# Self attentions of a decoder kernel: heads taken out with queries in rows, and a block of unread products

## The chip, the cores and the metric

The kernel runs on one core of one Trainium2 chip. The metric is the device time of one execution, in microseconds. The kernel before took 6091.39 us (median of three runs, 6082.24 to 6093.36). The profiled execution that the trace comes from took 6097.89 us, and its instructions span 6096.0 us of them.

## The reference

The program is a decoder of four layers over a batch of 16 sequences of 100 tokens with 128 features. Each layer is a self attention, a cross attention and a feed-forward part, each on the layernormed input and added to it. Only the four self attentions change. Each has 16 heads. Three of them (layers 0, 1, 3: `sa0`, `sa1`, `sa3`) have heads of 8 features and a causal mask; their core is the same:

```python
att = softmax(where(causal, einsum('bhqd,bhkd->bhqk', q, k) * scale, -inf))
y = einsum('bhqk,bhkd->bhqd', att, v)           # 8 features for each head
x = x + out_scale * (y.transpose().reshape(B, T, C) @ w_out + b)
```

The one of layer 2 (`sa2`) is a difference of two attentions over the same values, 16 features for each head, without a mask, and with a root mean square norm for each head:

```python
att = att1 - lam * att2
y = einsum('bhts,bhse->bhte', att, v)
y = y * rsqrt(mean(y * y, axis=-1) + 1e-5) * subln_w * (1 - LAMBDA_INIT)
x = x + y.transpose(0, 2, 1, 3).reshape(B, T, 2 * C) @ c_w.T
```

## The kernel before, in words

Activations lie with the 128 features in the partitions and tokens in the columns. A self attention goes through the 16 sequences in four groups G of four. A *unit* is one group and one softmax (`sa2` has two softmaxes, `sm` 0 and 1, so eight units; the others have four). A unit has eight *steps* t, one for each half (eight heads) of one sequence: 32 steps in `sa0`, `sa1`, `sa3`, 64 in `sa2`. The order on each engine is written out by hand, and semaphores tie the engines together.

In step t TensorE (all line numbers are those of the profile) puts the mask of step t + 3 into a score bank (`mask_scores`, L2751, causal stages alone), subtracts the row maxima of step t in banks 4 and 5 (`lower`, L2763 the transposed mask and L2764 the product with the diagonal of maxima), then does what `beside` names for this step, then the scores of step t + 3 (`score`, L2757) between those of step t with keys in rows (`scoreT`, L2770), four products that lie in different row groups and run side by side. VectorE takes the maxima of step t + 3 (L1818), GpSimd makes the diagonal of it (L951), and ScalarE takes the exponential of step t (L1260). Behind its scores TensorE does `values(t - 1)` (L2786): eight products that give, for each head, the weighted values and, by a column of ones, the sum of the weights. **The first instruction of step t + 1 waits for the exponential of step t** (`probsT_ready`): banks 4 and 5 are used again at once.

Two steps fill bank 6, one *slot* (a sequence): 16 heads in blocks of 32 partitions, 8 (or 16) rows of values and one row with the sum. ScalarE copies it to `o_sb` (`keep`, L1213). Then, in odd steps, `gathered` (L2795, four products whose stationary side is `o_sb` and whose moving side has 4 columns) turns the sums into a 100 x 16 tile in bank 7, VectorE inverts them (`inverse`, L1827), ScalarE writes each inverse 32 times (`widen`, L1227), and in even steps `spread` (L2804, four products of 128 x 100) brings the inverses back under their rows, where VectorE multiplies (`normalise`, L1837, L1839). `project` (L2820) is four products of 128 x 400 for a group, since the heads are spread over four blocks with gaps. In `sa2` the root mean square goes the same way: `squared` on ScalarE (L1218), `mean_squares` (L2795 again), `roots` (L1223), `widen_roots`, four `scale` for a group (L2804 again) and L1864 on VectorE. Value rows of the next group (L2740 the bias, L2741) are made in four steps of a unit, between `lower` and the scores. All these share bank 7, which goes back by `proj_free`.

The stage ends with a tail that has no scores of following steps: the last slots pass through `gathered`, `inverse`, `widen`, `spread` and `normalise` one after another, then the last `project` and `update` (L1874, L1876, L1878), which the next layernorm waits for. `sa1` also rounds its weights on VectorE before it starts (`quantise`, L1653), its output weight of 512 columns among them.

## Time and profile before

| | |
|---|---|
| median of three runs | 6091.39 us |
| profiled execution / its span | 6097.89 / 6096.0 us |
| TensorE busy | 4686.6 us (77%) |
| VectorE, ScalarE, GpSimd busy | 3317.4, 2411.6, 2210.9 us |
| `sa0`, GpSimd's diagonal of step 3 to that of step 31 | 81.02 to 232.93 us |
| `sa1`, the same | 1997.39 to 2110.84 us |
| `sa2`, step 3 to step 63 | 2655.21 to 2975.25 us |
| `sa3`, step 3 to step 31 | 4443.66 to 4573.51 us |

A busy TensorE is one that has a product under way; how fast the product goes depends on the clock that it is granted, which the profile gives as a share of full speed for each stretch (1.00 is 2.4 GHz, 0.50 is 1.2 GHz; it has no other level, so 0.72 is a mix in time). The chain of waits on the page has nothing on these stages; they are read from windows and from the timeline.

### The profile page before, as it was taken

To read this page: it belongs to the slowest core of one execution; us is meant where nothing else is said; L and a number is where in the kernel's file an instruction comes from. 1 tells how busy PE (TensorE), PEld (TensorE's weight loads), DVE (VectorE), ACT (ScalarE), POOL (GpSimd) and SP (SyncE) were. 2 spreads that over 40 slices of the span, in tenths; PEclk is the share of its full clock that TensorE was granted. 3 is DMA by queue.
4 is the path that set the end of the run, shared out by engine and by line. 5 is a ranking of instruction groups with operands and counts; after the bars stand their busy time and mean duration, and the time that the engine had idled before them with its cause. 6 is when DMAs were issued, how large, how long until landed. Compare 5 with 4: busy or idle time off the path is not lost. (4 is left out here: it accounts for less than half of the span.)

```text
span 6096.0 us, 84213 instructions
## 1 busy us (share of the span) xinstructions
PE 4686.6 (77%) x22350; PEld 3081.4 (51%) x22350; DVE 3317.4 (54%) x4953; ACT 2411.6 (40%) x3566; POOL 2210.9 (36%) x1247
## 2 busy tenths in 40 slices
PE   8899999999798966689878888888495444431698
PEld 4578888888544545346545555555252222220344
DVE  3344444444345322443266665664636999987344
ACT  2255555555222311233235555554133555540122
POOL 1256666555100300022146666664032555540000
PEclk6799999999799967775578998998686666655699
DMA  2000000000011022200021211110000000000011
GB/s 76 1 8 16 16 16 16 16 16 8 16 43 43 1 51 51 61 8 1 1 54 41 46 40 42 40 40 19 0 1 21 21 22 22 22 16 0 11 43 37
DMA packets 125094, 153.15 MB, mean 25 GB/s; under 512 B 87424, under 2 KB 110736, under 8 KB 124592
## 3 DMA queue, kind: packets, MB, share of 16 engines
q1 hardware_dynamic: 124720, 148.82, 10.0%
q8 instruction: 154, 2.52, 0.2%
q14 instruction: 220, 1.80, 0.1%
HBM read 110.42 MB, written 2.66 MB: 19 GB/s over the span
## 5 line engine op out<-in xcount | busy, mean ns | idle before, releaser
L1050 POOL TENSOR_TENSOR pexp_lo<-arena,pexp_hi 128x800 fp32r<-128x800 f32 x384 | 727.6, 1895 | 433.4 <-POOLq L1049 432.4
L1005 POOL TENSOR_TENSOR pexp_lo<-arena,pexp_hi 128x800 fp32r<-128x800 f32 x384 | 637.3, 1660 | 466.9 <-POOLq L1004 466.9
L2205 DVE TENSOR_REDUCE arena<-ps 100x1 f32<-100x482 f32 (+1 forms) x768 | 477.5, 656 | 235.7 <-DVEq L2174 223.3
L2060 DVE TENSOR_REDUCE arena<-ps 128x1 f32<-128x482 f32 (+3 forms) x624 | 392.8, 656 | 381.6 <-DVEq L2038 370.2
L1348 ACT ACTIVATE arena<-ps 128x800 f32<-128x800 f32 x384 | 322.3, 839 | 511.7 <-ACTq L1346 509.7
L1414 ACT ACTIVATE arena<-ps 128x800 f32<-128x800 f32 x384 | 321.8, 838 | 415.4 <-ACTq L1408 408.0
L951 POOL TENSOR_TENSOR max_diag<-w_const,arena 100x800 fp32r<-100x800 f32 x160 | 245.3, 1533 | 614.1 <-POOLq L949 614.1
L3202 PE MATMUL ps<-kst,qs 96*100 96x482 f32 (+1 forms) x768 | 338.3, 442 | 109.9 <-PEq L3162 105.7
L2512 DVE MATCH_REPLACE8 arena<-arena 100x1444 f32<-100x1444 f32 x256 | 420.3, 1652 | 0.0
L3440 PE MATMUL ps<-arena,chunk 128*128 128x400 f32 x648 | 285.2, 522 | 71.8 <-PEq L3439 71.1
L3344 PE MATMUL ps<-w_const,w_cross 100*128 100x100 f32 x192 | 43.2, 380 | 374.5 <-PEq L3341 374.5
L1818 DVE TENSOR_REDUCE arena<-ps 100x8 f32<-100x800 f32 x160 | 158.6, 992 | 307.0 <-DVEq L1815 306.8
L1349 ACT ACTIVATE pexp_hi<-ps 128x800 fp32r<-128x800 f32 x384 | 319.5, 832 | 0.0
L1415 ACT ACTIVATE pexp_hi<-ps 128x800 fp32r<-128x800 f32 x384 | 319.3, 832 | 0.0
L1089 POOL TENSOR_TENSOR arena<-arena 100x1444 f32<-100x1444 f32 x64 | 207.8, 3247 | 285.1 <-POOLq L1088 285.1
L2502 DVE MAX8 arena<-arena 100x8 f32<-100x1444 f32 x192 | 309.5, 1656 | 0.0
L2602 DVE TENSOR_TENSOR arena<-ps,arena 128x400 f32<-128x400 f32 x256 | 146.9, 574 | 293.5 <-DVEq L2593 184.4
L946 POOL MEMSET minus_ones<- 100x100 f32 x4 | 0.7, 182 | 833.7 <-POOLq L945 833.7
L1590 ACT ACTIVATE arena<-ps 128x400 f32<-128x400 f32 x256 | 129.0, 504 | 424.0 <-ACTq L1587 423.7
L3094 PE MATMUL ps<-pexp_hi,ctxk_hi 128*97 128x400 f32 (+1 forms) x768 | 281.2, 366 | 15.8 <-PEq L3089 15.6
L3432 PE MATMUL ps<-xn,chunk 128*128 128x400 f32 x648 | 278.6, 513 | 0.0
L3075 PE MATMUL ps<-qa_hi,ctxT_hi 113*128 113x400 f32 (+1 forms) x768 | 276.4, 360 | 1.4 <-PEq L3069 1.4
(365 smaller groups left out, 10880.3 us busy)
## 6 DMA issues: line engine op xcount, KB each, us to landing
ctxT<-in_ctxT SPq DMA_DIRECT2D x64, 541.5 KB
ctxk<-in_ctx SPq DMA_DIRECT2D x48, 528.0 KB
kst<-mid SPq DMA_DIRECT2D x128, 180.5 KB, 3.1
chunk<-in_ff_chunks SPq DMA_DIRECT2D x77, 193.0 KB, 2.4
arena<-gate_dram SPq DMA_DIRECT2D x64, 200.0 KB, 3.1
kst<-xn SPq DMA_DIRECT2D x64, 180.5 KB, 2.9
arena<-gate_dram SPq DMA_DIRECT2D x64, 100.0 KB, 2.6
w_cross<-in_ca SPq DMA_DIRECT2D x1, 3728.5 KB, 12.5
```

The source lines that it names most:

```text
L1005: own(nc.gpsimd.tensor_tensor(pexp_lo[p % 3][:, :, :], pexp[p % 3], pexp_hi[p % 3][:, :, :], ALU.subtract))
L1050: own(nc.gpsimd.tensor_tensor(pexp2_lo[p % 3][:, :, :], pexp2[p % 3], pexp2_hi[p % 3][:, :, :], ALU.subtract))
L1348: nc.scalar.activation(pexp[p % 3], of, ACT.Exp, scale=scale).then_inc(s.pexp_ready, 1)
L1349: own(nc.scalar.activation(pexp_hi[p % 3][:, :, :], of, ACT.Exp, scale=scale))
L1414: nc.scalar.activation(pexp2[p % 3], of, ACT.Exp, scale=scale).then_inc(s.pexp_ready, 1)
L1415: own(nc.scalar.activation(pexp2_hi[p % 3][:, :, :], of, ACT.Exp, scale=scale))
L2060: peak = nc.vector.tensor_reduce(mparts[0:at.stop - at.start, m, c:c + 1], bank(k, z - a, at.stop - at.start), AX.X, ALU.max)
L2205: peak = nc.vector.tensor_reduce(mparts2[:, h, c:c + 1], bank(k, z - a, S), AX.X, ALU.max)
L2502: nc.vector.max(tops[:, k, at], left[k]).then_inc(done[i], 1)
L2512: nc.vector.match_replace(left[k], tops[:, k, at], scores_sb[i] if r == 0 else left[k], TAKEN).then_inc(done[i], 1)
L3202: ins = mm(bank(k, z - a, S), qs[par][0:C, g, S * (h % 4):S * (h % 4) + S], kst[0:C, g, a:z], start=True, stop=True)
L3440: ins = mm(bank(4 + g), chunk[c][:, 256:384], h_all[k], start=False, stop=last)
```

## The change

The heads leave `o_sb` another way. `gathered` now has a moving side that picks all the rows, values and sum, of the four heads of a block: 36 columns for heads of 8 and 68 for heads of 16, so one set of four products gives a tile with the 100 queries in rows and, for each head, its features and its sum beside each other. VectorE inverts the sums and multiplies there. `inverse`, `widen` and `spread` are gone, and of `sa2` also `squared`, `mean_squares`, `widen_roots` and `scale`: squares, their sums, the product with the inverse roots and that with the weights are VectorE's, with queries in rows (`by_roots`, `by_weights`). For a group the result is turned back once (`features`, one set of four products for 128 features, so two in `sa2`), copied by ScalarE, and projected with one product (`sa2`: two). The output weight is 128 (256) columns wide, not 512. Value rows move behind `values` of even steps. In `sa2` these are steps 0, 2, 4, 6 of the units with `sm` 0. Ahead of step 0 of each stage TensorE does 14 products of 100 x 400 in bf16 (`unread`), which write banks 4 and 5 and are read by nobody.

```diff
-    own_block = i[:, None] // 32 == np.arange(4)[None, :]
+
+    def head_rows_of(n):
+
+        at = np.arange(4 * n)
+        return (i[:, None] == (at // n * 32 + at % n)[None, :]).astype(np.float32)
+
...
-                sum8=(own_block & (i[:, None] % 32 == 8)).astype(np.float32),
-                sum16=(own_block & (i[:, None] % 32 == 16)).astype(np.float32),
-                squares16=(own_block & (i[:, None] % 32 < 16)).astype(np.float32),
+                rows8=head_rows_of(9), rows16=head_rows_of(17),
...
@@ -628,38 +621,18 @@
     def beside(nsm, t):
 
         u, k = divmod(t, 8)
...
+        G, sm = u // nsm, u % nsm
+        if k % 2 == 0 and sm == 0 and G < NG - 1:
+            return "values", G + 1, k // 2
+        after = {(1, 0, 3): ("features", 0), (1, 0, 5): ("project", 0), (2, 0, 7): ("features", 0), (2, 1, 1): ("features", 1),
+                 (2, 1, 3): ("project", 0)}.get((nsm, sm, k))
+        return (after[0], G - 1, after[1]) if after and G > 0 else (None, 0, 0)
+
+    def step_behind(nsm, t):
+
+        return t % 16 if nsm == 2 and t >= 16 else -1
+
+    UNREAD_FIRST, UNREAD = 14, 0
...
+            def features(c):
+                act.wait_ge(s.proj_full, 1)
+                act.sem_inc(s.proj_full, -1)
+                nc.scalar.activation(y_feat[:, GT * c:GT * c + GT], bank(7), ACT.Copy).then_inc(s.act_done, 1)
+                act.wait_ge(s.act_done, 1)
+                act.sem_inc(s.act_done, -1)
+                act.sem_inc(s.proj_free, 1)
+                act.sem_inc(s.y_feat_ready, 1)
...
@@ -1817,54 +1766,39 @@
                 mx = smax[:, t % 3, :].rearrange("p (c h) -> p c h", c=2)
                 nc.vector.tensor_reduce(mx, sc, AX.X, ALU.max).then_inc(s.maxima_there, 1)
 
-            def norm_there():
+            def normalise(slot):
+
+                u, i = divmod(slot, 4)
+                G, sm, w = u // nsm, u % nsm, 16 * vw
+                y = y_tok[:, G % 2, w * i:w * i + w]
                 dve.wait_ge(s.norm_full, 1)
                 dve.sem_inc(s.norm_full, -1)
-
-            def inverse():
-
-                norm_there()
-                done(nc.vector.reciprocal(rden[:, :], bank(7, 16, S)))
-                dve.sem_inc(s.proj_free, 1)
-                dve.sem_inc(s.inverse_there, 1)
-
-            def normalise(slot):
-                u, i = divmod(slot, 4)
-                G, sm = u // nsm, u % nsm
-                y = y_rows[G % 2][:, :, i, :]
-                norm_there()
-                if sm == 0:
-                    done(nc.vector.tensor_tensor(y, o_sb[slot % 2], bs(bank(7)), ALU.mult))
-                else:
-                    done(nc.vector.tensor_tensor(second, o_sb[slot % 2], bs(bank(7)), ALU.mult))
-                dve.sem_inc(s.o_sb_free, 1)
+                o = bank(7, 16 * (vw + 1), S).rearrange("p (h w) -> p h w", w=vw + 1)
...
+                done(nc.vector.reciprocal(rden[:, :].unsqueeze(2), o[:, :, vw:vw + 1]))
+                r = rden[:, :].unsqueeze(2).to_broadcast([S, 16, vw])
+                to = y if sm == 0 else second
+                done(nc.vector.tensor_tensor(to.rearrange("p (h w) -> p h w", w=vw), o[:, :, 0:vw], r, ALU.mult))
                 dve.sem_inc(s.proj_free, 1)
                 if sm == 1:
-                    done(nc.vector.scalar_tensor_tensor(y, second, col[:, 6:7], y, ALU.mult, ALU.add))
-                    dve.sem_inc(s.rms_sum, 1)
+                    done(nc.vector.scalar_tensor_tensor(y, second, col[0:S, 6:7], y, ALU.mult, ALU.add))
+                    done(nc.vector.tensor_tensor(y_sq, y, y, ALU.mult))
+                    done(nc.vector.tensor_reduce(rms[:, 16 * i:16 * i + 16], y_sq.rearrange("p (h w) -> p h w", w=16), AX.X, ALU.add))
+                    if i == 3:
+                        dve.sem_inc(s.rms_sum, 1)
                 elif nsm == 1 and i == 3:
                     dve.sem_inc(s.y_ready, 1)
 
-            def mean_squares(i):
-                norm_there()
-                done(nc.vector.tensor_copy(rms[:, 16 * i:16 * i + 16], bank(7, 16, S)))
-                dve.sem_inc(s.proj_free, 1)
-                if i == 3:
-                    dve.sem_inc(s.rms_sum, 1)
-
-            def rms_inverse():
+            def by_roots(G):
+                y = y_tok[:, G % 2, :].rearrange("p (h w) -> p h w", w=16)
                 dve.wait_ge(s.rms_root, 1)
                 dve.sem_inc(s.rms_root, -1)
                 done(nc.vector.reciprocal(rms[:, :], rms[:, :]))
-                dve.sem_inc(s.inverse_there, 1)
-
-            def scale(G, i):
-                y = y_rows[G % 2][:, :, i, :]
-                norm_there()
-                done(nc.vector.scalar_tensor_tensor(y, y, subln[:, 0:1], bs(bank(7)), ALU.mult, ALU.mult))
-                dve.sem_inc(s.proj_free, 1)
-                if i == 3:
-                    dve.sem_inc(s.y_ready, 1)
+                done(nc.vector.tensor_tensor(y, y, rms[:, :].unsqueeze(2).to_broadcast([S, 64, 16]), ALU.mult))
+
+            def by_weights(G):
+                y = y_tok[:, G % 2, :].rearrange("p (h w) -> p h w", w=16)
+                done(nc.vector.tensor_tensor(y, y, subln[:, :].unsqueeze(1).to_broadcast([S, 64, 16]), ALU.mult))
+                dve.sem_inc(s.y_ready, 1)
 
...
@@ -2788,37 +2710,36 @@
                 if half == 1:
                     ins.then_inc(s.o_full, 1)
 
-            def gathered(of, which):
+            def gathered(slot):
 
                 side_bank()
+                n = 4 * (vw + 1)
                 for g in range(4):
-                    ins = mm(bank(7, 4, S, 4 * g), of[:, g, :], W("const", which), start=True, stop=True)
+                    ins = mm(bank(7, n, S, n * g), o_sb[slot % 2][:, g, :], W("const", "rows%d" % vw), start=True, stop=True)
                 ins.then_inc(s.norm_full, 1)
 
-            def spread(of):
-
+            def features(G, c):
                 side_bank()
-                pe.wait_ge(s.inverse_wide, 1)
-                pe.sem_inc(s.inverse_wide, -1)
-                for g in range(4):
-                    ins = mm(bank(7, S, 128, S * g), of[:, 128 * g:128 * g + 128], ident[0:S, 0:S], start=True, stop=True)
-                ins.then_inc(s.norm_full, 1)
-
-            def mean_squares():
-                pe.wait_ge(s.head_sq, 1)
-                pe.sem_inc(s.head_sq, -1)
-                gathered(y_sq, "squares16")
-
-            def scale(i):
-                spread(rms_wide[:, 512 * i:512 * i + 512])
-
-            def project(G):
+                if c == 0:
+                    pe.wait_ge(s.y_ready, 1)
+                    pe.sem_inc(s.y_ready, -1)
+                for i in range(4):
+                    at = 16 * vw * i + 128 * c
+                    ins = mm(bank(7, S, 128, S * i), y_tok[:, G % 2, at:at + 128], ident[0:S, 0:S], start=True, stop=True)
+                ins.then_inc(s.proj_full, 1)
+
+            def project():
                 side_bank()
-                pe.wait_ge(s.y_ready, 1)
-                pe.sem_inc(s.y_ready, -1)
-                for g in range(4):
-                    ins = mm(bank(7), wo[:, 128 * g:128 * g + 128], y_rows[G % 2][:, g, :, :], start=g == 0, stop=g == 3)
+                pe.wait_ge(s.y_feat_ready, nsm)
+                pe.sem_inc(s.y_feat_ready, -nsm)
+                for c in range(nsm):
+                    ins = mm(bank(7), wo[:, 128 * c:128 * c + 128], y_feat[:, GT * c:GT * c + GT], start=c == 0, stop=c == nsm - 1)
                 ins.then_inc(s.out_full, 1)
+
+            def unread(n):
+
+                for i in range(n):
+                    mm(bank(4 + i % 2, GT, S), id_bf, causal_bf[:, :], start=True, stop=True)
 
...
@@ -2848,6 +2769,8 @@
                 if t % 8 == 0:
                     pe.wait_ge(s.q_diag_ready, 1)
                     pe.sem_inc(s.q_diag_ready, -1)
+                if t % 8 == 0:
+                    unread(UNREAD if t > 0 else UNREAD_FIRST)
                 if more:
                     pe.wait_ge(s.scores_read, 1)
```

How the rows of TensorE stand in step 4 of `sa1` (an even step), before; the line numbers are those of each kernel's own text:

```order
L2764 MATMUL ps<-max_diag_49,minus_ones 100x400
L2741 MATMUL ps<-w_sa,xn 100x128
L2757 MATMUL ps<-arena 100x400
L2770 MATMUL ps<-arena 100x400
L2757 MATMUL ps<-arena 100x400
L2770 MATMUL ps<-arena 100x400
L2804 MATMUL ps<-w_const,arena 128x100 x4
L2786 MATMUL ps<-arena 32x100 x8
```

and now:

```order
L2686 MATMUL ps<-max_diag_50,minus_ones 100x400
L2679 MATMUL ps<-arena 100x400
L2692 MATMUL ps<-arena 100x400
L2679 MATMUL ps<-arena 100x400
L2692 MATMUL ps<-arena 100x400
L2708 MATMUL ps<-arena 32x100 x8
L2663 MATMUL ps<-w_sa,xn 100x128
```

L2757 is L2679 now (scores), L2770 is L2692 (scores with keys in rows), L2786 is L2708 (values), L2741 is L2663 (value rows), L2804 is `spread`. The value rows went from ahead of the scores to behind `values`, and `spread` is gone.

TensorE in step 13 of `sa1` (the odd step that projects group 0), before:

```order
L2764 MATMUL ps<-max_diag_50,minus_ones 100x400
L2763 MATMUL ps<-causalT_bf,ident_bf 100x400
L2764 MATMUL ps<-max_diag_50,minus_ones 100x400
L2820 MATMUL ps<-deviation,w_sa 128x400 x4
L2757 MATMUL ps<-arena 100x400
L2770 MATMUL ps<-arena 100x400
L2757 MATMUL ps<-arena 100x400
L2770 MATMUL ps<-arena 100x400
L2786 MATMUL ps<-arena 32x100 x8
L2795 MATMUL ps<-w_const,squares 100x4 x4
```

and now:

```order
L2686 MATMUL ps<-max_diag_50,minus_ones 100x400
L2685 MATMUL ps<-causalT_bf,ident_bf 100x400
L2686 MATMUL ps<-max_diag_50,minus_ones 100x400
L2736 MATMUL ps<-mid,w_sa 128x400
L2679 MATMUL ps<-arena 100x400
L2692 MATMUL ps<-arena 100x400
L2679 MATMUL ps<-arena 100x400
L2692 MATMUL ps<-arena 100x400
L2708 MATMUL ps<-arena 32x100 x8
L2718 MATMUL ps<-w_const,squares 100x36 x4
```

L2820 was four projection products and L2736 is one; L2795 was `gathered` with 4 moving columns and L2718 is the same with 36. The turn back (L2728, four products of 128 x 100) stands in step 11, at the place that the projection has here.

VectorE in `sa2`, two steps of a unit with `sm` 1, before (L1818 maxima, L1827 inverse, L1839 and L1843 the second softmax, L1850 the mean squares):

```order
L1839 TENSOR_TENSOR squares<-squares,ps 128x400
L1843 SCALAR_TENSOR_TENSOR deviation<-squares,col,deviation 128x4x100
L1818 TENSOR_REDUCE arena<-ps 100x8
L1827 RECIPROCAL arena<-ps 100x16
L1850 COPY arena<-ps 100x16
L1818 TENSOR_REDUCE arena<-ps 100x8
L1839 TENSOR_TENSOR squares<-squares,ps 128x400
L1843 SCALAR_TENSOR_TENSOR deviation<-squares,col,deviation 128x4x100
```

and now (L1767 maxima, L1777 inverse, L1780 and L1783 the second softmax, L1784 squares, L1785 their sums for each head):

```order
L1784 TENSOR_TENSOR deviation<-arena 100x256
L1785 TENSOR_REDUCE arena<-deviation 100x16
L1767 TENSOR_REDUCE arena<-ps 100x8 x2
L1777 RECIPROCAL arena<-ps 100x16
L1780 TENSOR_TENSOR squares<-ps,arena 100x256
L1783 SCALAR_TENSOR_TENSOR arena<-squares,col,arena 100x256
L1784 TENSOR_TENSOR deviation<-arena 100x256
L1785 TENSOR_REDUCE arena<-deviation 100x16
```

Where two steps had an inverse, two operations of 128 x 400 and a copy, they have an inverse and four operations on tiles of 100 x 256, one behind another.

## Rows read from the trace of the kernel before

**Rows 1.** The head of the page.
```profile
span 6096.0 us, 84213 instructions
```

**Rows 2.** Windows, diagonal 3 to last: stretch, us, PE, PEld, DVE, ACT, POOL, PEclk.
```profile
81.02:232.93 151.91, 147.99 (x1112) 89.69 (x1112) 46.78 (x69) 48.43 (x78) 42.69 (x29) 0.72 0.00 1
1997.39:2110.84 113.45, 106.36 (x1088) 68.51 (x1088) 48.61 (x67) 47.91 (x80) 42.70 (x29) 0.97 0.01 2
2655.21:2975.25 320.04, 307.32 (x2227) 195.14 (x2228) 118.33 (x183) 123.01 (x191) 91.47 (x60) 0.60 0.01 1
4443.66:4573.51 129.85, 123.16 (x1112) 75.73 (x1112) 49.24 (x69) 48.02 (x80) 42.70 (x29) 0.88 0.01 2
```

**Rows 3.** Windows: inside `sa0`, inside `sa1`, and twice inside `sa2`.
```profile
95.00:165.00 70.00, 69.94 (x404) 42.19 (x404) 15.78 (x24) 19.35 (x32) 15.25 (x10) 0.50 0.00 1
2010.00:2110.00 100.00, 95.07 (x996) 62.38 (x992) 45.08 (x61) 42.85 (x71) 38.12 (x25) 1.00 0.01 2
2666.00:2700.00 34.00, 31.00 (x369) 18.72 (x358) 20.56 (x27) 19.18 (x31) 15.74 (x11) 1.00 0.01 1
2705.00:2800.00 95.00, 91.75 (x635) 59.01 (x635) 33.35 (x54) 35.16 (x55) 25.76 (x17) 0.55 0.00 1
```

**Rows 4.** TensorE in `sa1` at 2.4 GHz: start, us, operation, tiles, count, [idle].
```profile
2060.34 0.51 PE L2751 MATMUL ps<-causal_bf,ident_bf 100*100 100x400 bf16 x2 [0.19 <-PEq L2853]
...
2062.35 1.14 PE L2804 MATMUL ps<-w_const,arena 100*128 100x100 f32 x8
...
2063.42 0.55 PE L2786 MATMUL ps<-arena 100*32 100x100 f32 x16
...
2066.64 0.87 PE L2795 MATMUL ps<-w_const,squares 128*100 128x4 f32 x8
...
2067.54 0.51 PE L2751 MATMUL ps<-causal_bf,ident_bf 100*100 100x400 bf16 x2
```

**Rows 5.** TensorE in `sa0` at 1.2 GHz, the timeline.
```profile
126.24 1.50 PE L2795 MATMUL ps<-w_const,squares 128*100 128x4 f32 x8
...
127.60 0.89 PE L2751 MATMUL ps<-causal_bf,ident_bf 100*100 100x400 bf16 x2
...
131.35 2.03 PE L2804 MATMUL ps<-w_const,arena 100*128 100x100 f32 x8
```

**Rows 6.** TensorE in `sa2` at 1.2 GHz, the timeline.
```profile
2854.07 0.97 PE L2764 MATMUL ps<-max_diag,minus_ones 100*100 100x400 f32 x2
...
2856.57 2.03 PE L2804 MATMUL ps<-w_const,arena 100*128 100x100 f32 x8
...
2859.35 0.99 PE L2764 MATMUL ps<-max_diag,minus_ones 100*100 100x400 f32 x2
```

**Rows 7.** ScalarE in `sa1`: the first exponential's table, and a later exponential.
```profile
1996.15 1.28 ACT L1260 ACT_TABLE_LOAD   x1 [3.46 <-ACTq L1259]
...
2062.61 0.84 ACT L1260 ACTIVATE arena<-ps 100x800 f32<-100x800 f32 x1 [1.05 <-ACTq L1259]
```

**Rows 8.** TensorE in `sa1`: step 1, and the last projection inside the steps.
```profile
1998.58 0.51 PE L2751 MATMUL ps<-causal_bf,ident_bf 100*100 100x400 bf16 x2 [2.60 <-PEq L2853]
...
2111.75 2.92 PE L2820 MATMUL ps<-deviation,w_sa 128*128 128x400 f32 x8
```

**Rows 9.** VectorE in `sa2`: an update beside GpSimd's work, maxima, an update alone.
```profile
2696.66 1.25 DVE L1843 SCALAR_TENSOR_TENSOR deviation<-squares,col,deviation 128x400 f32<-128x400 f32 x1 [0.33 <-DVEq L1763]
...
2708.93 0.99 DVE L1818 TENSOR_REDUCE arena<-ps 100x8 f32<-100x800 f32 x1 [1.82 <-DVEq L1815]
...
2976.85 0.63 DVE L1843 SCALAR_TENSOR_TENSOR mid<-squares,col,mid 128x400 f32<-128x400 f32 x1 [0.33 <-DVEq L1763]
```

**Rows 10.** VectorE: the last update of `sa1`, and that of `sa2`.
```profile
2138.24 0.57 DVE L1878 TENSOR_TENSOR x<-ps,x 128x400 f32<-128x400 f32 x1 [5.29 <-DVEq L1871]
...
3037.83 0.57 DVE L1878 TENSOR_TENSOR x<-ps,x 128x400 f32<-128x400 f32 x1 [6.27 <-DVEq L1871]
```

**Rows 11.** VectorE, rounding the output weight of `sa1`.
```profile
1976.71 0.69 DVE L1675 TENSOR_TENSOR w_sa<-squares,w_sa 128x512 f32<-128x512 f32 x1
```

168 lines of the change are left out of this document (41 added, 127 removed).

## The prediction

> **What bounds the kernel now.** The head of the page comes first: the span is 6096.0 us [rows 1] of the 6097.9 that the profiled execution took, and the median of the runs is 6.5 us below that. The chain of waits has nothing on the self attentions, so I cut each of them out by windows, from GpSimd's diagonal of step 3 to its last one: 28 steps in `sa0`, `sa1`, `sa3`, 60 in `sa2`. They take 151.9, 113.5, 129.9 and 320.0 us [rows 2]. Three stages with the same instructions differ by a third, and the column beside them tells why: the granted clock is 0.72, 0.97 and 0.88, and 0.60 in `sa2`. TensorE is busy for 94 to 97% in all four, while VectorE, ScalarE and GpSimd are busy for less than half. So TensorE sets the pace, and what it costs depends first on its clock.
>
> Smaller windows show the two levels apart [rows 3]. `sa0` from 95 to 165 is at 1.2 GHz (0.50) with TensorE busy for 69.94 of 70 us. `sa1` from 2010 to 2110 is at 2.4 GHz (1.00) with 95.07 of 100. `sa2` is at 2.4 GHz from 2666 to 2700, then at 0.55 for the next 95 us. A full engine is thus no guard of the clock.
>
> Now one step. At 2.4 GHz two steps of `sa1` go from mask to mask in 2067.54 - 2060.34 = 7.20 us, of which `spread` is 1.14, `values` 0.55 and `gathered` 0.87 [rows 4]. At 1.2 GHz mask to `spread` is 131.35 - 127.60 = 3.75 us instead of 2.01, `spread` 2.03, `gathered` 1.50 [rows 5]. In `sa2` at 1.2 GHz a step with `spread` is 2859.35 - 2854.07 = 5.28, and 2.50 of it lie ahead of `spread` [rows 6].
>
> There is a second limit just below TensorE's work, a ring: step t + 1 may not begin before the exponential of step t ends. The exponential starts 2062.61 - 2060.34 = 2.27 us behind the mask and takes 0.84; from an exponential's end to the next mask is 1998.58 - (1996.15 + 1.28 + 0.84) = 0.31 us [rows 7, 8]. The ring is 3.42 us, whatever TensorE has left to do.
>
> **The change part by part.** I work out each stage at either clock, then choose the clock.
>
> Even causal steps lose `spread` and get value rows behind `values`. Mask to the end of the scores is 2.01 and `values` 0.55: 2.56 us, so 0.86 us are free ahead of the ring's 3.42, and value rows (a product of 100 x 128, with the bias two) lie inside them. Odd steps keep 2.01 + 0.55 and `gathered`, now of 36 columns. It has no row; between 0.87 (4 columns) and 1.14 (100 columns, `spread`) it is 0.96 by proportion, together 3.5. A pair of steps is 6.9 us. 14 pairs are 97. For each of three groups one turn back (as `spread`, 1.14) and one projection product (a quarter of 2.92 [rows 8], 0.73) add 5.6. With 1.3 for the first exponential's table, which lies in the window, a causal stage at 2.4 GHz is 104 us. At 1.2 GHz the ring is 3.75 + 0.26 + 0.84 + 0.31 = 5.16, an odd step 3.75 + 0.83 (between 0.55 and its double) + 1.68 = 6.26; 14 pairs are 160, with 3 x 3.5 and the table 172 us.
>
> The clock. `sa1` is at 2.4 GHz already, and its steps stay as dense: -9.5. In `sa0` the clock rises only past 165, behind the first projection of four wide products, which the change takes away; in its place 14 wide products without a wait between them stand ahead of the steps. I take it that they raise the clock at the start, as the projection did, and that steps with 0.86 us idle in 6.9 hold it, as `sa1` held it with 5 us idle in 100 [rows 3]: `sa0` 104 (-48), `sa3` 108 with a piece at 1.2 (-22). This is the choice that weighs most, and the bounds are 104 and 172 for each stage.
>
> The Trainium skill ("TensorE: Matmul & The Clock Gate", "What's actually happening") says that the throttled clock is the default and that activity releases it. [...]
>
> The block itself: two masks are 0.51 us at 2.4 [rows 4] and 0.89 at 1.2 [rows 5], so 14 products are 3.6 or 6.2 us. TensorE may be waiting there anyway for the first diagonal; each stage pays 0 to 6.2. I take 3.7 and 15 for four.
>
> `sa2` at 1.2 GHz: the ring is 2.50 + 0.26 + 0.84 + 0.31 = 3.91, an odd step with `gathered` of 68 columns (1.50 to 2.03, 1.85) is 2.50 + 0.83 + 1.85 = 5.18. 60 steps at 4.55 are 273; six turns back (12.2) and three double projections (each half of four products at half the clock, 2.92, 8.8), 294; with 9 for three changes of ScalarE's tables for the root (1.28 a load [rows 7], two loads each and what waits for them), 303. At 2.4 GHz the ring without masks is 3.42 - 0.51 = 2.91 and units with `sm` 0 run at 3.0. In those with `sm` 1 VectorE may be the bound: two maxima (0.99 each), an inverse, and four operations on 256 columns. One of 400 takes 1.25 us beside GpSimd's work and 0.63 alone [rows 9], so one of 256 is 0.4 to 0.8; with 0.33 of wait ahead of each of five, two steps are 5.5 to 7.1, and I take 3.6 for one. On average 3.3: 198, with turns, projections and tables 219. Its clock falls now at 2700 while it is well filled, and the change makes its steps no denser, nor has it a block later than the first. I take one part in five at 2.4 GHz, as 0.60 says now: 0.8 x 303 + 0.2 x 219 = 286, that is -34, between 0 (all at 1.2 with VectorE late in its `sm` 1 units) and -101.
>
> "SBUF — State Buffer", "Who interferes with whom", of the Trainium skill says that VectorE's operations with two inputs in SBUF and GpSimd's lock each other out. The trace agrees, 1.25 against 0.63 us; it bears on three of the new operations in two steps of `sm` 1.
>
> The tails. `sa1` goes from 2110.84 to the last update, 2138.81 [rows 10], 28.0 us. Twice an inverse, a widening, `spread` (1.14) and their hand-overs stand in it, and a projection of 2.92. A `spread` with a ScalarE operation and two hand-overs of 0.3 is about 2.3; both go, the projection loses 2.2, and a turn back with its copy costs 2.1: -4.7; at the clocks of the other stages up to -9. I take -6.5, -7.5, -7.5, in all -22 (bounds -12 and -28). `sa2` takes 3038.40 - 2975.25 = 63.1. Four rounds of `scale` (2.03 + 0.63 + 0.6 = 3.3) and of squares with their gathering (1.50 + 0.84 + 0.6 = 2.9) go, 25 us, and operations on VectorE of 0.4 to 1.6 come, seven of them, while a chain of widening goes: -25 with bounds -15 and -35.
>
> The output weight is rounded in 128 columns instead of 512: one such operation takes 0.69 [rows 11]; of five, three quarters go, -2 (0 if the stage's start waits for something else).
>
> Sum: -48 - 9.5 - 22 - 34 - 22 - 25 - 2 + 15 = -147.5. 6097.9 - 147.5 is 5950.4, and with the 6.5 us that the median lies below the profiled execution, 5944. What is late next is the exponential in even causal steps, TensorE in odd ones and in `sa2`.
>
> **The rivals.**
>
> A, the forecast: 5944.
>
> B, `sa2` also holds 2.4 GHz. For it: its steps lose the long thin products, as `spread`, and it held the level for 34 us with the table and VectorE's work as they are. Against: it lost it behind a filled stretch, and gets no block there. It gives 219 instead of 286: 5877.
>
> C, one causal stage does not rise or falls back. For it: `sa0` stands at 0.50 for 70 us with a full engine, and its projection, behind which the clock rose, is gone; the first exponential's table leaves TensorE 2.60 us idle [rows 8] right behind the block in `sa1` and `sa3`. Against: `sa1` rose by itself at 2007, `sa3` at 4475 without any projection. 172 instead of 104: 6012; for two of them 6080.
>
> D, slower: none of the four holds the clock, since the ring now leaves 0.86 us idle in each even step and 2.60 behind the block. It decides at the granted clock of steps 1 to 8: at 0.50 there, nothing later lifts it. 3 x 68 - 4 for `sa3`, 17 in `sa2`, and 2.5 more for each block: 5944 + 227 = 6171, 80 over the median of before. `sa1`, at 1.00 with the same ring, speaks against it.
>
> E, the change does not do what it says for the clock: block and denser work leave it as it is in each stage. At the mix of 0.72 (44 parts in 100 at 2.4 GHz) `sa0` is 1 / (0.44/104 + 0.56/172) = 133, `sa3` at 0.88 in the same way 115: 36 more than A, 5980. If also VectorE takes all of `sa2`'s gain (34) and the tails stay at their low bounds (20), 6034. For it: `sa1` and `sa3` rose with what they have, so the block may only come early. Against: nothing that I can read.
>
> **How the numbers follow.** A 0.48, own range 5910 to 5980; B 0.20; C 0.17; E 0.10; D 0.05. The range leaves out D, two stages of C and what lies under B: 5865 to 6030. 0.2% is 12 us, about what a measurement of this kernel can tell from no change. Faster is A, B, C and most of E: 0.92; within 0.2% 0.03 (two stages of C with a tail at its bound); slower 0.05, D.
>
> **What the profile after would show.** Windows as in rows 2: 104, 104, 286 and 108 us at 1.00, 1.00, 0.60 and 0.95. Mask to mask over two causal steps 6.9 us, even steps with 0.9 us idle ahead of the mask and an exponential as its releaser, `gathered` 0.96 at 2.4 GHz. The block 3.6 us long and behind it 2.60 idle in `sa1`. In `sa2` `gathered` 1.05 or 1.85, VectorE's share above the 37% of now (118.33 of 320.04), most in `sm` 1. Tails 21.5 and 38 us. I am wrong if a causal stage stands at 0.50 past its step 8 (C, D), if `sa2` is above 0.8 (B), or if VectorE is what ends TensorE's waits in `sa2`.

## The result, and the profile after

The changed kernel takes 5865.53 us (median of four runs, 5842.36 to 5872.14) against 6092.38 for the one before: the ratio is 0.9617, with a 95% interval of 0.9581 to 0.9653. That is faster by some 227 us where 147 were forecast. The direction, the causal stages and the tails came out as worked out or somewhat better; one term, the clock of `sa2`, was mis-sized by most of the difference. It is close to rival B (5877). The median lies at the very edge of the range (5865), and 0.9617 of the 6091.39 that the forecast started from is 5858, just below it.

The profiled execution took 5872.14 us. The head of its page:

```profile
span 5870.4 us, 81917 instructions
```

Windows of the kernel after, from the diagonal of step 3 to the last, `sa0`, `sa1`, `sa2`, `sa3`. The columns are the stretch, its us, the busy time of TensorE, its weight loads, VectorE, ScalarE and GpSimd, then the granted clock. They answer to [rows 2].

```profile
83.77:183.59 99.82, 94.76 (x1018) 57.11 (x1017) 42.10 (x69) 41.12 (x68) 42.69 (x29) 1.00 0.01 2
1928.97:2033.60 104.63, 94.86 (x996) 56.43 (x996) 41.01 (x67) 40.43 (x71) 42.69 (x29) 0.95 0.01 2
2593.56:2822.00 228.44, 193.16 (x1895) 103.48 (x1896) 126.64 (x196) 93.25 (x145) 93.70 (x61) 0.81 0.01 1
4255.73:4356.94 101.21, 94.88 (x1018) 57.27 (x1018) 42.09 (x69) 41.16 (x71) 42.69 (x28) 1.00 0.01 2
```

The stages are shorter by 52.1, 8.8, 91.6 and 28.6 us, 181.1 together. In `sa2` read the busy time and the clock together. TensorE was idle for 12.7 of 320.0 us before (320.04 - 307.32) and is for 35.3 of 228.4 now, and yet its clock went from 0.60 to 0.81. An engine with nearly three times the idle time got the higher clock.

The last updates on VectorE, `sa1` and `sa2`, answer to [rows 10]:

```profile
2051.53 0.57 DVE L1812 TENSOR_TENSOR x<-ps,x 128x400 f32<-128x400 f32 x1 [5.20 <-DVEq L1805]
...
2849.79 0.57 DVE L1812 TENSOR_TENSOR x<-ps,x 128x400 f32<-128x400 f32 x1 [9.39 <-DVEq L1805]
```

From the last diagonal these tails are 17.9 us (27.4 to the same point before) and 27.8 (62.6), so 9.5 and 34.8 us less. The tails of `sa0` and `sa3` are 18.8 us (30.6 before) and 19.6 (29.6), so 11.8 and 10.0 less. Stages and the tails of `sa1` and `sa2` make 225 us, as much as the spans differ; the blocks at the starts, the other two tails and what differs between the stages about cancel. Among these is a thing that the change does not touch: the cross attention and the feed-forward part between `sa1` and `sa2` took 509.8 us before and 534.7 now.

```profile
2138.24:2648.03 509.79, 329.65 (x1403) 224.70 (x1403) 173.59 (x321) 80.67 (x168) 26.83 (x34) 0.72 0.21 51
```

is the window of the kernel before, and of the one after:

```profile
2051.53:2586.24 534.71, 355.82 (x1403) 244.29 (x1403) 173.52 (x321) 80.62 (x168) 26.81 (x33) 0.66 0.19 48
```

The same 1403 products at 0.66 instead of 0.72 took 25 us more. In the run e1 below, with the same code there, the stretch took 509.5 us. Over all the profiles of this document it falls into two groups: 508 to 510 us at 0.72 (the kernel before, e1, e2, e6, e9) and 531 to 536 us at 0.66 or 0.67 (all others). All three profiles with the steps of before are in the first group, and only two of the eleven with the new steps; whether that is chance or comes from what stands ahead of the stretch, no run here tells. One profile of a kernel is therefore read stage by stage, and a stage's time has some chance in it.

TensorE of the kernel after in `sa1` at 2.4 GHz, an even and an odd step: start, us, line, tiles, and the idle time before it in brackets. They answer to [rows 4].

```profile
1986.70 0.51 PE L2673 MATMUL ps<-causal_bf,ident_bf 100*100 100x400 bf16 x2 [0.22 <-PEq L2776]
...
1989.18 0.46 PE L2663 MATMUL ps<-w_sa,xn 128*100 128x128 f32 x2
1990.09 0.51 PE L2673 MATMUL ps<-causal_bf,ident_bf 100*100 100x400 bf16 x2 [0.44 <-POOLq L923]
...
1992.57 0.90 PE L2718 MATMUL ps<-w_const,squares 128*100 128x36 f32 x8
1993.51 0.51 PE L2673 MATMUL ps<-causal_bf,ident_bf 100*100 100x400 bf16 x2
```

The last diagonal on GpSimd and the exponential on ScalarE that stand ahead of the second mask, and a mask behind an even step that makes no value rows:

```profile
1986.59 1.52 POOL L924 TENSOR_TENSOR max_diag<-w_const,arena 100x800 fp32r<-100x800 f32 x1 [1.86 <-POOLq L922]
1988.96 0.84 ACT L1211 ACTIVATE arena<-ps 100x800 f32<-100x800 f32 x1 [2.76 <-ACTq L1210]
...
2019.08 0.51 PE L2673 MATMUL ps<-causal_bf,ident_bf 100*100 100x400 bf16 x2 [0.84 <-POOLq L923]
```

Mask to mask is 3.39 us for the even step and 3.42 for the odd one: 6.81 for both, where 7.20 stood and 6.9 was forecast. `gathered` with 36 columns takes 0.90 us; with 4 it took 0.87. Nine times the columns go through for 0.03 us more. Keep this pair in mind for e9 below.

The block, once in `sa0`, where it starts at the lower clock, and once in `sa1`:

```profile
75.06 4.91 PE L2742 MATMUL ps<-causal_bf,ident_bf 100*100 100x400 bf16 x14
...
1923.12 2.54 PE L2742 MATMUL ps<-causal_bf,ident_bf 100*100 100x400 bf16 x14 [0.21 <-PEq L2771]
```

And in `sa2` the first place behind its start where its clock falls, ScalarE's table loads around the root first:

```profile
2650.97 1.28 ACT L1197 ACT_TABLE_LOAD   x1 [0.46 <-ACTq L1196]
...
2652.63 1.28 ACT L1211 ACT_TABLE_LOAD   x1
```

and TensorE's rows there, `gathered` of step 3 of group 1 and `lower` of step 4:

```profile
2651.24 0.92 PE L2718 MATMUL ps<-w_const,squares 128*100 128x68 f32 x8
2655.21 0.96 PE L2686 MATMUL ps<-max_diag,minus_ones 100*100 100x400 f32 x2 [3.04 <-PEq L2783]
```

Behind an idle time of 3.04 us the same `lower` takes 0.96 us instead of 0.58: the engine is at 1.2 GHz. The falls of units 4 and 6 stand at 3.41 and 3.38 us of the same kind. The fall behind the first root lasts 7 us, those behind the second and the third 37 us each: windows of unit 4 and unit 5, around the second.

```profile
2690.72:2718.32 27.60, 22.02 (x242) 11.20 (x241) 21.68 (x31) 14.50 (x22) 12.97 (x9) 0.89 0.01 2
2718.32:2757.68 39.36, 36.42 (x270) 20.54 (x269) 14.43 (x25) 11.95 (x19) 12.19 (x8) 0.60 0.00 1
```

### The profile page after: what moved, and what is told of

Same layout as the page of the kernel before. It is cut to its first block and busy times, and to the rows that moved or that the text cites. A ratio compares the mean times of both kernels' runs of the same rounds, so it can differ in the third digit from the quotient of the medians.

```text
span 5870.4 us, 81917 instructions
## 1 busy us (share of the span) xinstructions
PE 4451.6 (76%) x21582; PEld 2913.4 (50%) x21582; DVE 3299.6 (56%) x4961; ACT 2348.7 (40%) x3474; POOL 2212.0 (38%) x1247
## 5 line engine op out<-in xcount | busy, mean ns | idle before, releaser
L1767 DVE TENSOR_REDUCE arena<-ps 100x8 f32<-100x800 f32 x160 | 158.3, 991 | 248.2 <-DVEq L1764 248.1
```

## The experiments

My theory before the first of them: the block brings the clock up at each start, the denser steps hold it, and in `sa2` the absence of `spread` and its like (thin products: 100 columns and fewer for each stationary side) keeps it up. The rivals: the steps need no block; the clock of `sa2` hangs on the root's tables; the place of the value rows. Stage times below are the same windows as above, from one profile of each kernel; medians and ratios are from the timed runs.

**e1, without the block.**

```diff
-    UNREAD_FIRST, UNREAD = 14, 0
+    UNREAD_FIRST, UNREAD = 0, 0
```

> The changed kernel without the 14 unread products. Theory 1 (the block brings the clock up at each stage's start, the denser steps hold it): sa0 has nothing that lifts it and stays at 1.2 GHz for most of its 28 steps, about 170 us instead of 99.8; sa3 comes late as before, 20 us more; sa1 and sa2 alike within 10; in all +80 to +110 us over 5865, less 11 for four blocks. Theory 2 (the denser steps lift the clock by themselves): sa0 within 115 us, the whole within 20 us of the changed kernel, or faster by the 11 us that the blocks take.

5841.06 us, ratio 0.9578 (0.9527 to 0.9628). Windows of `sa0` and `sa2`:

```profile
80.93:186.75 105.82, 101.15 (x1018) 59.97 (x1018) 42.09 (x69) 41.38 (x69) 42.68 (x29) 0.93 0.01 2
...
2574.84:2785.27 210.43, 172.86 (x1874) 92.26 (x1870) 126.63 (x195) 92.50 (x145) 95.56 (x60) 0.89 0.01 2
```

Theory 1 falls: `sa0` rises without the block, at 96 us by the profile's record of the granted clock, and loses 6 us, not 70. `sa3` takes 102.9.

**e2, the kernel before with the block alone.**

```diff
                 if t % 8 == 0:
                     pe.wait_ge(s.q_diag_ready, 1)
                     pe.sem_inc(s.q_diag_ready, -1)
+                if t == 0:
+                    for n in range(14):
+                        mm(bank(4 + n % 2, GT, S), id_bf, causal_bf[:, :], start=True, stop=True)
```

> The kernel before with the block of 14 alone ahead of each stage. Theory 1 (block lifts, what streams through the array holds): sa0 is lifted at its start and, since it held 2.4 GHz for units 2 and 3 with the same steps, keeps it: about 115 to 120 us instead of 151.9; sa3 about 117 instead of 129.9; sa2 falls at its first roots as now, 320 give or take 15: 6045 to 6055. Theory 2 (the block is worth nothing without the denser steps): within 10 us of 6091.

6061.2 us, ratio 0.9933 (0.9899 to 0.9967). `sa0`, `sa2` and `sa3`:

```profile
83.88:201.29 117.41, 110.22 (x1112) 69.24 (x1112) 49.34 (x69) 48.03 (x78) 42.67 (x29) 1.00 0.01 2
...
2633.77:2947.16 313.39, 299.83 (x2231) 191.71 (x2232) 119.68 (x184) 122.81 (x191) 91.42 (x60) 0.63 0.01 1
4416.20:4547.35 131.15, 123.66 (x1112) 76.10 (x1112) 49.32 (x69) 47.83 (x80) 42.67 (x28) 0.88 0.01 1
```

With the steps of before the block does work in `sa0` (117.4 instead of 151.9), as theory 1 has it. `sa2` gains little, 313.4 for 320.0. In `sa3` (131.2 for 129.9) the sum hides two things, the first and the last unit:

```profile
4400.32:4440.16 39.84, 35.17 (x240) 19.36 (x236) 10.11 (x14) 11.74 (x21) 12.19 (x9) 0.76 0.01 1
...
4511.55:4547.35 35.80, 34.82 (x266) 21.12 (x264) 9.62 (x14) 10.06 (x15) 10.66 (x7) 0.67 0.01 1
```

Before they took 46.24 us at 0.52 and 25.41 at 1.00. So the block lifted `sa3` early too, and then its clock fell for 24 us in the last unit, where TensorE has no idle time of even 1 us. So block and new steps each come with a mended `sa0`; their gains don't add.

**e3, no table change in `sa2`.** A copy stands in place of the square root of the mean squares.

```diff
-                nc.scalar.activation(rms[:, :], rms[:, :], ACT.Sqrt, bias=eps_col(0)[0:S], scale=1 / 16)
+                nc.scalar.activation(rms[:, :], rms[:, :], ACT.Copy, scale=1 / 16)
```

> The changed kernel whose square root of the mean squares in sa2 is left out (a copy stands in its place, so ScalarE loads no other table inside the steps). Theory 1 (the clock of sa2 falls because TensorE stands idle for 3.04 us behind the two table loads of 1.28 us each, as at 2652): sa2 is at 1.00 from its second unit on, about 200 us instead of 228, the tail shorter by 3 to 5, in all -30 to -35. Theory 2 (the clock falls by VectorE's load in units with sm 1 or by itself): the loads' own time goes, 3 x 3 us and 3 in the tail, -10 to -13, and the clock stays near 0.81.

5856.75 us, ratio 0.9588 (0.9542 to 0.9634). `sa2`:

```profile
2603.47:2815.53 212.06, 180.46 (x1896) 97.39 (x1896) 123.35 (x196) 84.33 (x139) 93.60 (x60) 0.87 0.01 2
```

Neither theory's number. The idle times of over 3 us are gone and the falls behind them too, but the clock then falls elsewhere, twice in unit 3 and once each in units 5, 6 and 7; the longest idle times there are 1.0 to 1.2 us, and one of 1.14 us in unit 1 brought none. So the long idle times are not the only end of the high clock. What they cost in all this run can't tell: r1 below has the tables and takes 207.6 us.

**e4, thin products in even steps** of all stages, where `spread` was.

```diff
+                if t % 2 == 0 and t >= 4:
+                    side_bank()
+                    for g in range(4):
+                        ins = mm(bank(7, S, 128, S * g), ident[0:S, :], ident[0:S, 0:S], start=True, stop=True)
+                    ins.then_inc(s.proj_free, 1)
                 if t > 0:
                     values(t - 1)
```

> The changed kernel with four unread products of 128 x 100 in each even step from step 4 on, where spread stood, in bank 7. Theory 1 (removing spread is what gives sa2 its clock, since little streams through the array in it): sa2 is back at 0.60 to 0.65 and takes 280 us or more instead of 228; causal stages keep 1.00 and gain at most the 0.3 us by which an even step then passes the ring, 4 to 5 us each. Theory 2 (sa2's clock comes from the shorter stage or the missing scale and squares): sa2 stays at 0.8 and takes 228 + 29 x 0.3 = 237; the whole 20 us more.

5897.15 us, ratio 0.9651 (0.9604 to 0.9699). `sa2`:

```profile
2612.94:2853.01 240.07, 224.43 (x2116) 136.96 (x2120) 126.69 (x196) 96.37 (x144) 93.58 (x60) 0.82 0.01 2
```

Against the first profile of the changed kernel theory 2 holds: 240.1 for 228.4 us with the clock where it was. `spread` cost its own time, 9.1 us in `sa0` (108.9), 8.6 in `sa3`, 12 in `sa2`, more than I gave it, since a step that holds it is longer than the ring. But against the second profile, r1 below (207.6 at 0.93), `sa2` is 32.5 us longer and its clock lower, and e7 below says the same beside e1. So whether thin products in every second step lower the clock of `sa2` is open; by these later profiles they do.

**e5 and e6, thin or wide in every step of `sa2`.** The pair differs in what the engine does for the same time.

```diff
+                if nsm == 2 and (t >= 16 or t >= 4 and t % 2 == 0):
+                    side_bank()
+                    for g in range(4):          # e5
+                        ins = mm(bank(7, S, 128, S * g), ident[0:S, :], ident[0:S, 0:S], start=True, stop=True)
+                    for g in range(6):          # e6 instead
+                        ins = mm(bank(7, GT, S), id_bf, causal_bf[:, :], start=True, stop=True)
+                    ins.then_inc(s.proj_free, 1)
```

> The changed kernel with four unread products of 128 x 100 (thin, as spread, scale and the gathering of squares were) in sa2 alone: in each even step of its first two units and in every step from 16 on, in bank 7. Theory 1 (few columns through the array for the time that they hold it: that is what kept sa2 of before at 1.2 GHz): sa2 at 0.65 or less and 290 us or more instead of 228. Theory 2 (they only cost their own time, 1.0 to 1.2 us, less what was idle): sa2 stays at about 0.8; 62 sets cost at most 70 us at that mix, of which 0.9 for each even step is free: 255 to 265.

> The same, with six unread products of 100 x 400 bf16 (1.09 us at 2.4 GHz by the block's 2.54 for 14) where e5 has four thin ones: the same engine time, but 2400 columns in place of 400. Theory 1 (what streams decides): sa2 stands at 0.95 or more and never falls for long; about 24.5 us for units 0 and 1, 31 for the others: 230 to 240 in spite of 62 blocks more. Theory 2 (busy time decides, not what the engine is busy with): the same clock and time as e5 within 10 us.

e5: 5904.46 us, ratio 0.9697 (0.9653 to 0.9742), `sa2`:

```profile
2605.71:2886.38 280.67, 270.52 (x2289) 174.43 (x2290) 117.87 (x196) 96.37 (x144) 93.54 (x61) 0.74 0.01 1
```

e6: 5853.16 us, ratio 0.9608 (0.9569 to 0.9648), `sa2`:

```profile
2574.65:2805.60 230.95, 220.18 (x2187) 122.06 (x2188) 117.36 (x196) 96.38 (x144) 93.54 (x61) 0.96 0.01 2
```

And unit 3 of each, e5 first:

```profile
2680.30:2730.55 50.25, 49.70 (x349) 33.03 (x348) 14.10 (x24) 12.16 (x19) 12.18 (x9) 0.59 0.00 1
...
2645.99:2678.53 32.54, 31.59 (x326) 18.36 (x314) 13.92 (x24) 12.16 (x19) 12.18 (x8) 1.00 0.00 1
```

This is the cleanest of the results. TensorE is busy for 96% in e5 and 95% in e6, the sets stand at the same places, and the stage with thin ones is 50 us longer; the medians of the whole differ by 51, and no run of e6 is as long as the shortest of e5 (5864.72 and 5888.33). Units 3, 5 and 7, which have them in each step and the heavier VectorE, take 50.3, 50.1 and 43.6 us with thin ones (clock 0.59 to 0.63) and 32.5, 32.9 and 30.1 with wide ones (1.00). The falls begin at the same places, the roots of units 2, 4 and 6; what differs is how long they last: 51, 48 and 38 us in e5, none, 7 and 7 in e6 (each also has one of 7 at the stage's start). Of e5's theories the second's price was too low and the first's too high: 281, between 265 and 290, at a clock of 0.74 between 0.65 and 0.8. In e6 theory 1 holds to the number, and 54 sets of work that nobody reads (the expectation of e5 has 62, which is a miscount) cost 2.5 us against the changed kernel's 228.4, and 23.4 against the 207.6 of r1. The pair doesn't say which property of the thin ones matters: they have fewer columns, but also another number type (fp32 for bf16) and more weight loads (174 us busy for 122). The columns alone are changed in e9.

**e7, thin products in even steps and no block,** the edits of e1 and e4 together.

> The changed kernel without the block, and with four unread thin products in even steps of all stages, where spread stood: the run without the block rose in sa0 at 96 us, the run with block and thin products held what it had. Theory 1 (spread's absence lets sa0 rise by itself): sa0 now stays at 1.2 GHz until group 1 or later, 140 us or more instead of 105.8, sa3 120 or more. Theory 2 (value rows, projection or the gathering let it rise): sa0 rises near 96 us again, at most 118 us.

5895.62 us, ratio 0.9676 (0.9634 to 0.9718). `sa0`:

```profile
80.77:195.36 114.59, 113.53 (x1120) 72.21 (x1120) 42.11 (x69) 42.56 (x68) 42.68 (x29) 0.93 0.01 2
```

It rises at 95.7 us again, so `spread` did not hold `sa0` down. Theory 2. In `sa2` the thin products take 27.3 us over e1's 210.4, at 0.81 for 0.89:

```profile
2614.08:2851.82 237.74, 222.45 (x2098) 136.10 (x2098) 126.24 (x195) 96.22 (x144) 94.63 (x61) 0.81 0.01 2
```

**e8, the block behind the root's tables,** and at a start in `sa0` alone.

```diff
-                if t % 8 == 0:
-                    unread(UNREAD if t > 0 else UNREAD_FIRST)
+                if t == 0 and cfg.get("gate") or step_behind(nsm, t) == 4:
+                    unread(14)
```

> The changed kernel with the block in sa0 alone of the four starts, and three more blocks of 14 in sa2 right behind the 3.04 to 3.41 us for which TensorE stands idle for the root's tables. Theory 1 (that idle is what drops the clock and a block brings it back at once): sa2's pieces at 1.2 GHz are 7 us each, the stage is 200 + 3 x 3.5 = 205 to 215 us instead of 228; three blocks at the starts saved, 8 to 10: 5830 to 5845. Theory 2 (the clock falls again by the steps themselves in units with sm 1): sa2 225 or more.

5856.14 us, ratio 0.962 (0.9578 to 0.9661). `sa2`:

```profile
2591.74:2806.26 214.52, 177.18 (x1916) 96.43 (x1912) 124.63 (x195) 92.07 (x145) 95.51 (x60) 0.92 0.01 2
```

214.5 is theory 1's number, and the falls behind the three roots lasted 3.4, 3.4 and 6.8 us; but one of 20.5 us began at 2625, ahead of the first root, and the whole is no better than the changed kernel. What it shows is less than it seems, as the repetition below tells.

**e9, the kernel before with a wider `gathered`:** 36 (68) columns stream where 4 did, and the 32 (64) more are read by nobody; each product overwrites them, so that the sums stand where they stood.

```diff
+                at, w = where["const"][which][1], {"sum8": 36, "sum16": 68}.get(which, 4)
                 for g in range(4):
-                    ins = mm(bank(7, 4, S, 4 * g), of[:, g, :], W("const", which), start=True, stop=True)
+                    ins = mm(bank(7, w, S, 4 * g), of[:, g, :], packed["const"][:, at:at + w], start=True, stop=True)
```

> The kernel before, whose gathering of sums streams 36 (68) columns instead of 4 in each of its four products; only the first 4 are read. Theory 1 (the wide gathering is what lets sa0 of the changed kernel rise by itself at 96): sa0 rises near 96 instead of 167, its window is 120 us or less instead of 151.9, sa3 gains as much as sa0 or less. Theory 2 (it is the place of the value rows or the missing waits of the chain of inverses): sa0 stays at 0.5 to about 165 and takes 2 to 4 us more.

6038.45 us, ratio 0.993 (0.9894 to 0.9965). `sa0`, `sa2`, `sa3`:

```profile
80.68:201.77 121.09, 115.15 (x1112) 71.28 (x1112) 49.24 (x69) 48.10 (x78) 42.69 (x29) 0.96 0.01 2
...
2627.17:2896.74 269.57, 248.92 (x2227) 156.43 (x2228) 128.32 (x183) 122.13 (x191) 91.49 (x61) 0.78 0.01 2
4352.97:4505.62 152.65, 147.74 (x1112) 89.50 (x1112) 47.00 (x69) 48.23 (x80) 42.68 (x28) 0.72 0.01 1
```

With an edit that only adds work, 0.03 us for a set, `sa0` is 30.8 us shorter and `sa2` 50.5, and the clock of `sa2` goes from 0.60 to 0.78 with not one instruction fewer. The whole is 0.7% faster, and its interval leaves out 1. `sa0` rises at 91.5 us. `sa3` speaks against it: it rose 100 us behind its first diagonal instead of 45, at the end of its second unit, and lost 22.8. Theory 1 for `sa0`, and not for `sa3`. These are single profiles of programs whose times spread widely (6055 to 6129 us in 13 runs of the kernel before, 6012 to 6098 in ten of e9). For `sa2` there is a second profile with the narrow set, e2's, and it agrees with the first (313.4 us at 0.63). For `sa0` without a block there is none, so its part may be chance.

**e10, without the block, value rows of group 0 back ahead of the scores** in causal stages.

```diff
+        if nsm == 1 and G == 0:
+            at = {1: 0, 3: 1, 4: 2, 6: 3}
+            return ("values", 1, at[k]) if k in at else (None, 0, 0)
         if k % 2 == 0 and sm == 0 and G < NG - 1:
             return "values", G + 1, k // 2
...
+                elif kind == "values" and nsm == 1 and t < 8:
+                    side_bank()
+                    value_rows(G, i, 7)
                 if more:
                     score(t + 3, 0)
```

> The changed kernel without the block, whose value rows of group 0 in the causal stages stand where they stood before, in steps 1, 3, 4 and 6 ahead of the scores. Theory 1 (the wide gathering lifts): sa0 rises near 96 us as without this edit, 105 to 110 us. Theory 2 (the place of the value rows lets it rise): sa0 is at 1.2 GHz up to its second group, 125 us or more.

5884.88 us, ratio 0.9673 (0.9627 to 0.9718). `sa0` and `sa3`:

```profile
79.90:186.96 107.06, 100.23 (x1022) 59.61 (x1022) 42.12 (x69) 41.35 (x69) 42.69 (x29) 0.95 0.01 2
...
4245.88:4366.13 120.25, 113.20 (x1022) 66.05 (x1022) 42.01 (x69) 41.34 (x71) 42.69 (x28) 0.82 0.01 1
```

`sa0` rises at 90.6: the place of the value rows is not what lets it. `sa3`, with nothing but the place of four pairs of products changed, rose 56 us behind its first diagonal instead of e1's 19 and took 17.4 us more than e1's 102.9. With e9 that makes two cases in which `sa3` came up late, both with the wide `gathered`; what decides when it rises is not shown.

**r1 and r2, the changed kernel and e1's kernel once more,** on one chip, in five rounds.

> The changed kernel once more, on one chip with the next run, for what its block is worth in all: 6 us gained in sa0, 3 to 4 paid in each of sa1, sa2, sa3. Theory 1 (the block is worth nothing in all): the two medians differ by less than 12 us. Theory 2 (it costs more than it brings, since where it falls sets the clock later): this one is 20 us or more above the next.

> The changed kernel without the block once more, beside the run before. Theory 1: within 12 us of it. Theory 2: 20 us or more below it, sa2 at 0.85 or more again.

5856.83 us (0.9625, 0.9588 to 0.9662) with the block and 5853.23 (0.9622, 0.9585 to 0.9659) without. Theory 1: the block is worth nothing in the whole. The 24 us by which e1 seemed better than the changed kernel are not there when both run on one chip. And `sa2` of r1, the same program as the changed kernel:

```profile
2605.54:2813.09 207.55, 169.36 (x1896) 89.96 (x1896) 127.29 (x196) 92.75 (x145) 93.70 (x60) 0.93 0.01 2
```

207.6 us and 0.93, where the first profile had 228.4 and 0.81: the 20.9 us between them are the size of chance in one `sa2`. In `sa0` of the kernel without block it was 105.8 and then 99.8, no longer than with it:

```profile
80.98:180.74 99.76, 94.76 (x1018) 57.09 (x1017) 42.12 (x69) 41.12 (x68) 42.69 (x28) 1.00 0.01 2
```

## Why the prediction came out as it did

*The bound, and the causal stages: right.* 99.8, 104.6 and 101.2 us stand where 104, 104 and 108 were forecast; the pair of steps is 6.81 for 6.9 and `gathered` 0.90 for 0.96. The ring is as I had it, 3.39 us for 3.42. An even step without value rows leaves 0.84 us idle, for 0.86; one with them leaves 0.44, since they take 0.46 of it, and the forecast of 0.9 idle ahead of the mask in every even step forgot that it had put them there. What ends that time is the exponential, as forecast. It ends at 1988.96 + 0.84 = 1989.80, and the mask starts 0.29 us later, for 0.31. The profile names GpSimd there (L923, which gives a score bank back), but by the order of the program the bank that this mask needs was given back ahead of the diagonal at 1986.59, 3.5 us earlier.

*What lifts `sa0`: right in the time, wrong in the reason.* "I take it that they raise the clock at the start": e2 shows that 14 wide products can. But e1, e7 and e10 rise without them, r2 stands at 1.00 as early as with them, and r1 against r2 shows no worth of them in the whole (3.6 us, within what such runs can tell). The argument that `sa0` needs a riser because its projection is gone overlooked that the new steps are not the old ones. e9 points at what in them does it, the 32 columns more in `gathered`; as the same edit left `sa3` at 1.2 GHz for longer, that is likely and not shown.

*`sa2`: here the prediction failed.* The step is "the change makes its steps no denser", and the term built on it, one part in five at 2.4 GHz. The forecast was 286; it took 228.4 and 207.6, at 0.81 and 0.93, which is 6 to 9 parts in ten. The second is even below the 219 that was the bound for all of it at 2.4 GHz. Two parts of the change put more through the engine in the time that it is busy. `gathered` streams 68 columns in 0.92 us where 4 of `sa1` took 0.87; alone it brings 50.5 of the 91.6 us (e9, one profile). And the thin products of `scale`, `spread` and the mean squares, a set or two in each step, are gone; put back as one in each step, they cost 52.2 us against the first profile and 73.1 against the second (e5), while as much time of wide ones costs 2.5 and 23.4 (e6). I had counted both by their engine time alone, though the first thing I had read, `sa0` at 0.50 with a full engine [rows 3], said that engine time is not what the clock goes by. With the measured clock of 0.81 my own two prices give 0.38 x 303 + 0.62 x 219 = 251, so the clock makes 35 of the 58 us of error, and steps cheaper than I had them the other 23 (r1's 0.93 gives 231 in the same way, again 23 over the measured time): at 2.4 GHz unit 1, with `sm` 1, runs at 24.06 / 8 = 3.0 us for a step.

```profile
2610.66:2634.72 24.06, 19.45 (x243) 10.24 (x244) 14.01 (x24) 10.62 (x17) 12.20 (x8) 1.00 0.01 2
```

*VectorE in `sm` 1.* I took 3.6 us for a step as its bound; unit 3 took 27.60 / 8 = 3.45 with its turn back and projection, unit 1 3.0, with VectorE busy for 14.01 of its 24.06 us. That is near the ring's 2.91, so VectorE didn't set the pace there. The price of one operation was right (0.42 us for three of the four in most cases, 0.49 for the other at its shortest), and one beside GpSimd's diagonal could be above my 0.8:

```profile
2629.46 0.67 DVE L1783 SCALAR_TENSOR_TENSOR arena<-squares,col,arena 100x256 f32<-100x256 f32 x1 [0.24 <-DVEq L1712]
...
2647.76 1.81 DVE L1783 SCALAR_TENSOR_TENSOR arena<-squares,col,arena 100x256 f32<-100x256 f32 x1 [0.24 <-DVEq L1712]
```

This is the mutual exclusion of which the Trainium skill tells ("SBUF — State Buffer", "Who interferes with whom"). The trace agrees, with 0.67 us where a diagonal covers the first 0.38 of them (2628.32 to 2629.84), and 1.81 beside one of 1.52 us that starts at 2647.77: both end 0.29 us behind the diagonal. It bears on two of the four operations and not on three as I wrote: L1783 and L1784 have both inputs in SBUF, while L1780 reads one from a bank and was never longer than 0.43 us.

*The tails:* -9.5 for -6.5 in `sa1`, -11.8 and -10.0 for -7.5 each in `sa0` and `sa3`, so -31 in all, past the bound of -28; and -34.8 for -25 in `sa2`, at its bound of -35. I had what turn back and projection save at the end too low. The 2 us for the rounding of the output weight were not followed up. *The blocks:* 4.91 us at the lower clock in `sa0` and 2.54 in `sa1`, where 3.7 was taken for each; from the first diagonal to that of step 3 the four starts are 7.3 us longer in all, not 15.

*The rivals.* B (0.20) is the nearest to what happened, though `sa2` doesn't hold 2.4 GHz throughout: it falls at each root and comes back. D, that idle gaps bring the clock down, is refuted for gaps of a step: `sa1` is idle for 9.8 of 104.6 us, and its units behind the first stand at 1.00. It holds for long ones in `sa2`, which fell with each of 3.04, 3.41 and 3.38 us (and once for 7 us at its start). In the profiles of the changed kernel and its variants there are 22 idle times of 2.97 to 3.50 us in `sa2`, and a fall begins with each of them or within 1.4 us of its end. In between the record is mixed: behind 2.20 us ahead of step 1 `sa1` fell for 10 us, and behind the same 2.20 us in e6 it didn't. The Trainium skill ("TensorE: Matmul & The Clock Gate", "Why this matters for your kernels") warns of long idle gaps between bursts of products, and the trace agrees. It also asks to keep TensorE busy; that can't be the busy time of the profile alone, for e5 and e6 have the same, at 0.74 and 0.96.

*Open:* what lets `sa0` rise early, why e9 and e10 came up late in `sa3`, why a fall in `sa2` lasts 7 us in one place and 37 in another of the same run, and how the 41 us of `sa2` that e9 doesn't explain (62 against r1) divide between thin products and waits that went with them. The exact measure by which the chip grants its clock was not looked for.

## What to carry to other kernels

Where TensorE sets the pace, read the granted clock of each stage ahead of its busy share, and price an edit by what it puts through the array too: a set of four products of 4 columns costs as much time as one of 36 and can cost the stage its clock. Replacing thin products (a few columns for each stationary side) by wide ones, or widening them with columns that nobody reads, may bring more than taking instructions away. A block of unread products at the start helped a stage whose steps held the clock and reached it late (`sa0` in e2); steps that reach it by themselves didn't need it, and the first thing to look for after that is an idle time of 3 us, such as a change of ScalarE's tables. Judge such edits by several runs on one chip, and a stage by more than one profile: a second profile of the same program moved a stage of 228 us by 21, and with it what e3, e4 and e8 seemed to say.

## What the runs showed of the hardware

- Columns and time of a small product: 4 columns 0.87 us, 36 columns 0.90, 68 columns 0.92 for eight passes at 2.4 GHz.
- A kernel with more work can be a little faster: e9 adds columns alone and has a ratio of 0.993 (0.9894 to 0.9965).
- Six unread products of 400 columns in 54 of 60 steps of `sa2` (e6) leave the stage at 231.0 us, against 228.4 and 207.6 without them.
- Thin and wide sets of the same engine time, at the same places: falls of the clock last 51, 48 and 38 us with thin ones (e5) and none, 7 and 7 with wide ones (e6).
- Idle times of TensorE of 2.97 to 3.50 us in `sa2`: all 22 came with a fall to 1.2 GHz, of 3.4 to 44 us; 2.20 us ahead of step 1 in `sa1` came with one in the changed kernel and with none in e6.
- The clock of a stretch that no edit touched has two values over the profiles: 508 to 510 us at a granted clock of 0.72 in five of them, 531 to 536 us at 0.66 or 0.67 in nine.
